# Attention head outputs taken through DRAM to feature rows, softmax sums inverted once per eight heads, in an attention and mixture-of-experts kernel

## The reference, cut to what matters

```python
x = x + attention(layernorm(x))          # x is 2 x 2048 x 256 fp32
x = x + experts(layernorm(x))

def attention(x):                        # 16 heads of 16 features
    Q, K, V = (x @ W.T + b for W, b in (q, k, v))      # split into heads
    A = softmax(Q @ K.T / 4)             # 2048 x 2048 for each of 32 (sequence, head) pairs
    L = local_diffusion_kernel(2048, 0.4)              # a band: |i - j| <= 3, rows sum to 1
    out = (0.6 * A + 0.4 * L) @ V        # heads side by side again: 2048 x 256 a sequence
    return out @ Wo.T + bo

def experts(x):                          # router: 256 -> 512 -> 4, gelu, softmax, the best 2 of 4
    for e in range(4):                   # each token is weighed by its gate of expert e, 0 if not chosen
        out += gate[e] * (gelu(x @ We1[e] + be1[e]) @ We2[e] + be2[e])     # 256 -> 1024 -> 256
```

## Time and profile before

| | |
|---|---|
| median of 3 runs | 1970.37 us (1968.87 to 1970.62) |
| the profiled execution's own time | 1970.84 us |
| its span | 1969.0 us, mean granted TensorE clock 0.996 |
| busy | TensorE 98%, VectorE 83%, ScalarE 68%, GpSimd 18% |

### The profile page before, as it was taken

One profiled execution on the slowest core, in us unless ns is written; L12 is line 12 of the kernel. 1 busy time (PEld: TensorE's weight loads), 2 busy tenths in 40 slices (PEclk: granted clock), 3 DMA queues, 4 the chain that ended last, 5 costly groups with the idle time before them and its releaser, 6 DMA issues. The chain is left out here.

```text
span 1969.0 us, 47293 instructions
## 1 busy us (share of the span) xinstructions
PE 1934.3 (98%) x16220; PEld 1025.6 (52%) x16220; DVE 1642.2 (83%) x2235; ACT 1338.4 (68%) x2374; POOL 346.1 (18%) x379
## 2 busy tenths in 40 slices
PE   7999999999999999999999999999999899999997
PEld 3543333333333333333333333333587799999997
DVE  6799999999999999999999999996156765555554
ACT  3348888888888888888888888888545422223332
POOL 1362010000000010001000000001025622322233
PEclk9999999999999999999999999999999999999999
DMA  8954345434553455435543455342024787888884
GB/s 260 253 121 93 76 97 102 102 75 87 102 112 75 78 102 111 85 75 97 103 101 75 88 101 112 75 78 72 28 71 149 270 253 231 255 250 299 261 273 116
DMA packets 117242, 264.07 MB, mean 134 GB/s; under 512 B 20001, under 2 KB 68257, under 8 KB 110497
## 3 DMA queue, kind: packets, MB, share of 16 engines
q1 hardware_dynamic: 104016, 245.29, 49.4%
q0 software_dynamic: 13152, 17.83, 4.7%
HBM read 206.95 MB, written 73.94 MB: 143 GB/s over the span
## 5 line engine op out<-in xcount | busy, mean ns | idle before, releaser
L618 DVE TENSOR_REDUCE part_max<-psum 128x1 f32<-128x1024 f32 x1024 | 1214.9, 1214 | 13.8 <-PE psum L725 3.2
L686 ACT ACTIVATE probs<-psum 128x512 f32<-128x512 f32 x2048 | 1110.3, 595 | 166.5 <-PE psum L740 108.7
L740 PE MATMUL psum<-score_q,score_k 50*128 50x512 f32 x2048 | 756.9, 448 | 0.1
L725 PE MATMUL psum<-max_k,max_q 48*128 48x512 f32 x2048 | 731.4, 449 | 1.4 <-DVE part_max L618 1.4
L750 PE MATMUL psum<-probs,v_ones 128*32 128x256 f32 x8192 | 654.2, 391 | 0.5 <-ACT probs L686 0.5
L740 PEld LDWEIGHTS psum<-score_q,score_k 50*128 50x128 f32 x2048 | 309.0, 184 | 426.3 <-ACT probs L686 398.1
L750 PEld LDWEIGHTS psum<-probs,v_ones 128*32 128x32 f32 x8192 | 161.2, 108 | 369.9 <-issue 204.4
L725 PEld LDWEIGHTS psum<-max_k,max_q 48*128 48x128 f32 x2048 | 291.2, 185 | 15.8 <-issue 7.0
L1137 ACT ACTIVATE x_sb<-psum,x_sb 128x512 f32<-128x512 f32 (+1 forms) x160 | 101.5, 635 | 254.2 <-PE psum L1517 252.0
L1536 PE MATMUL psum<-w,h_hi 128*128 128x256 f32 x1120 | 202.7, 279 | 0.0
L1536 PEld LDWEIGHTS psum<-w,h_hi 128*128 128x128 f32 x1120 | 179.2, 189 | 10.8 <-issue 0.4
(11 more groups left out here) (177 smaller groups left out, 1301.6 us busy)
## 6 DMA issues: line engine op xcount, KB each, us to landing
w<-w_split SPq DMA_DIRECT2D x40, 2048.0 KB, 8.6
max_q<-qk_pieces SPq DMA_DIRECT2D x192, 128.0 KB, 7.1
score_k<-qk_pieces SPq DMA_DIRECT2D x192, 128.0 KB, 4.6
xs<-in_pads SPq DMA_DIRECT2D x33, 528.0 KB, 7.9
qk_pieces<-pieces SPq DMA_DIRECT2D x32, 512.0 KB, 5.0
w_split<-w_pair SPq DMA_DIRECT2D x32, 512.0 KB, 8.4
max_k<-qk_pieces SPq DMA_DIRECT2D x192, 64.0 KB, 7.8
score_q<-qk_pieces SPq DMA_DIRECT2D x192, 64.0 KB, 2.2
```

What stands on the lines that cost most here:

```text
L618: nc.vector.tensor_reduce(part_max[:, t, p:p + 1], ps_m[p].rearrange("q b f -> q (b f)"), axis=AXIS.X, op=ALU.max).then_inc(m_read, 1)
L686: nc.scalar.activation(probs[kb % 2][:, chunk * BLOCK:(chunk + 1) * BLOCK], score_bank(u, kb, c), ACT.Exp, scale=float(HD) ** -0.5).then_i ...
L725: last = nc.tensor.matmul(ps_m[p][:, h, :], max_q[u][rows, t * P:(t + 1) * P], max_k[u][rows, p * BLOCK:(p + 1) * BLOCK], start=True, stop ...
L740: nc.tensor.matmul(score_bank(u, kb, c), score_k[u][rows, kb * P:(kb + 1) * P], score_q[u][rows, part * BLOCK:(part + 1) * BLOCK], start=T ...
```

## The change

The output bank of a head is no longer transposed. VectorE copies it to `heads_sb` (128 x 512). SyncE stores that to DRAM (`o_raw`) and loads it back with two DMAs: the 16 rows of outputs to 16 partitions of `o_sb`, whose rows are now features (128 partitions, for eight heads, x 2048 queries), and the 16 rows of sums to the same partitions of `sums`. When eight heads are in, VectorE inverts `sums` in place and GpSimd multiplies `o_sb` by it. The factor 0.6 moves into the ones, which become 1/0.6. Three of the four inversions are in heads 9, 17 and 25, in four pieces of 512 columns after tiles 2, 4, 6 and 8. The fourth is in the routing, one piece of 2048 columns. The four matmuls with `jump` for each bank give way to one bf16 matmul of zeros, 32 rows x 512 columns, that opens the bank. VectorE adds the heads to the mixed bank while it takes it out (`add_heads`), where ScalarE copied before. The shift's transposes go in two pieces, after tiles 11 and 12. The queries of Q are no longer permuted, and are stored in runs of 512 elements. The loops over heads of SyncE and VectorE are unrolled.

```diff
-SHIFT_AT = 12
+SHIFT_AT = 11
+GROUP = HEADS // KD
+    INVERT_AT = (2, 4, 6, 8)
...
+def store_out(sp, dram, keep, n):
+    sp.wait_ge(keep["o_copied"], n + 2)
+    sp.dma_start(dram["o_raw"][n], keep["heads_sb"]).then_inc(keep["o_stored"], 16)
+
+def load_out(sp, dram, keep, n):
+    rows = slice((n % GROUP) * HD, (n % GROUP + 1) * HD)
+    sp.wait_ge(keep["o_stored"], 16 * (n + 2))
+    held = n // GROUP
+    if n % GROUP == 0 and held > 0:
+        sp.wait_ge(keep["o_normal"], held)
+    raw = dram["o_raw"][n].rearrange("(j e) q -> e j q", j=BPS)
+    for dst, src in ((keep["o"][rows, n // GROUP, :], raw[0:HD]), (keep["sums"][rows, :], raw[HD:2 * HD])):
+        sp.dma_start(dst.rearrange("p (j q) -> p j q", j=BPS), src).then_inc(keep["o_in"], 16)
+
+def invert_sums(nc, dve, keep, g, piece, pieces):
+    dve.wait_ge(keep["o_in"], 16 * 2 * GROUP * (g + 1))
+    part = keep["sums"][:, piece * SEQ // pieces:(piece + 1) * SEQ // pieces]
+    done = nc.vector.reciprocal(part, part)
...
+def normalise_out(nc, pool, keep, g):
+    pool.wait_ge(keep["o_inverted"], g + 1)
+    heads = keep["o"][:, g, :]
+    nc.gpsimd.tensor_tensor(heads, heads, keep["sums"], ALU.mult).then_inc(keep["o_normal"], 1)
...
-    for t in range(BT):
-        nc.tensor.matmul(out[:, t * P:(t + 1) * P], o[:, kt + t, :], keep["jump"][:], start=t == 0, stop=False)
+    nc.tensor.matmul(out, zeros[:, 0:P], zeros[:, P:P + BLOCK], start=True, stop=False)
...
-                            if qk == 0:
-                                rows = rows.rearrange("p (b j r) -> p j b r", b=BT, j=BPS)
...
# attend, SyncE
-        twice(sp, pairs, body)
+        for n in range(NHEADS):
...
+            if n > 0:
+                store_out(sp, dram, keep, n - 1)
+                load_out(sp, dram, keep, n - 1)
+            if n + 1 < NHEADS:
+                sp.wait_ge(shift_turned, n + 2)
+                load_shift(1 - u)
...
# attend, GpSimd
             split_chunk(n)
-            normalise(n)
             if n + 1 < NHEADS:
                 split_shift(n + 1)
+            if n > GROUP and n % GROUP == 1:
+                normalise_out(nc, pool, keep, n // GROUP - 1)
...
# attend, VectorE
-            nc.vector.transpose(heads_tok[:].rearrange("p t e -> p (t e)"), out_bank(u)).then_inc(heads_turned, 1)
+            nc.vector.tensor_copy(heads_sb, out_bank(u)).then_inc(o_copied, 1)
...
+                if n > GROUP and n % GROUP == 1 and kb in INVERT_AT:
+                    invert_sums(nc, dve, keep, n // GROUP - 1, INVERT_AT.index(kb), len(INVERT_AT))
...
+                    if kb == SHIFT_AT:
...
+                        turn_shift(n + 1, (0, 1))
+                    if kb == SHIFT_AT + 1:
+                        turn_shift(n + 1, (2, 3))
...
# route_and_experts, SyncE: ahead of the constants
+        store_out(sp, dram, keep, NHEADS - 1)
+        load_out(sp, dram, keep, NHEADS - 1)
...
# route_and_experts, GpSimd
+            if i == 1:
+                normalise_out(nc, pool, keep, NHEADS // GROUP - 1)
...
# route_and_experts, VectorE
+        def add_heads(i):
+            b, at = i // BPS, (i % BPS) * BLOCK
+            dve.wait_ge(o_normal, KD * (b + 1))
+            if i > 0:
+                dve.wait_ge(o_ready, i)
+            for m in range(KD):
+                dve.wait_ge(a_ready[m], i + 1)
+                nc.vector.tensor_tensor(attnT[:, m, :], ps_a[m], o_sb[:, KD * b + m, at:at + BLOCK], ALU.add
+                                        ).then_inc(a_copied[m], 1)
...
+        add_heads(0)
         normalise(0)
+        add_heads(1)
...
                 normalise(i + 1)
+                if i + 2 < BLOCKS:
+                    add_heads(i + 2)
+                if i == 0:
+                    invert_sums(nc, dve, keep, NHEADS // GROUP - 1, 0, 1)
```

More of the change, by code:

```diff
@@ L628, in split_shift, with turn_shift, copy_out @@
             dve.wait_ge(shift_step, m + 1)
-        def turn_shift(m):
-            dve.wait_ge(shift_ready, m + 1)
+        def turn_shift(m, quads):
             rows = shift[:].rearrange("p h c t -> p (h c t)").bitcast(F32)
-            for q in range(0, P, QUAD):
-                last = nc.vector.transpose(shift_row[:, q:q + QUAD], rows[q:q + QUAD, :])
-            last.then_inc(shift_turned, 1)
-        def turn_heads(n, u):
-            dve.wait_ge(pv_done, ST * (n + 1) + PV_OPEN)
-            dve.wait_ge(tok_used, n + 1)
-            nc.vector.transpose(heads_tok[:].rearrange("p t e -> p (t e)"), out_bank(u)).then_inc(heads_turned, 1)
-        def invert(n):
-            dve.wait_ge(heads_turned, n + 1)
-            nc.vector.reciprocal(inv_sum[:], heads_tok[:, :, HD]).then_inc(inv_ready, 1)
+            for q in quads:
+                turned = nc.vector.transpose(shift_row[:, q * QUAD:(q + 1) * QUAD], rows[q * QUAD:(q + 1) * QUAD, :])
+            if q == P // QUAD - 1:
+                turned.then_inc(shift_turned, 1)
+        def copy_out(n, u):
+            dve.wait_ge(o_stored, 16 * (n + 1))
+            dve.wait_ge(pv_done, ST * (n + 1) + PV_OPEN)
+            nc.vector.tensor_copy(heads_sb, out_bank(u)).then_inc(o_copied, 1)
         for t in range(ST):
-            maxima(t, t)
+            for p in range(2):
+                maxima(t, t, p)
         split_shift(0)
@@ L1084, in _ @@
     def _(act):
-        def copy_heads(i):
-            for m in range(KD):
-                act.wait_ge(a_ready[m], i + 1)
-                if m == 0 and i > 0:
-                    act.wait_ge(o_ready, i)
-                nc.scalar.activation(attnT[:, m, :], ps_a[m], ACT.Copy).then_inc(a_copied[m], 1)
         def copy_hi(i):
@@ L1098, in exponentials @@
             nc.scalar.activation(prob[:], below_top[:], ACT.Exp).then_inc(exp_ready, 1)
-        for i in range(3):
-            copy_heads(i)
-            if i == 1:
-                copy_hi(0)
+        copy_hi(0)
         def split_x(i):
@@ L1609, in program @@
                 keep["v"] = head_sb("v_sb", [P, BATCH, ST + 2, HEADS, HD])[:]
[L1610 to L1611 removed]
+                keep["o"] = head_sb("o_sb", [P, BATCH * KD, SEQ])[:]
+                keep["sums"] = head_sb("sums", [P, SEQ])[:]
+                keep["heads_sb"] = head_sb("heads_sb", [P, BLOCK])[:]
+                for n in ("o_copied", "o_stored", "o_in", "o_inverted", "o_normal"):
+                    keep[n] = sem(n)
                 for n, toks in (("max_q0", SEQ), ("max_k0", SPLIT)):
```

159 lines of the change are left out of this document (69 added, 90 removed).

## The result

The changed kernel takes 2045.07 us, median of 4 runs (2041.68 to 2052.29), against 1969.78 us of the kernel before on the same chip: a ratio of 1.0387, 95% interval [1.0358, 1.0416]. That is 75 us more where 38 were forecast, above the end of the range (2028).

A forecast was written before the change was run, and what follows sets the result against it. TensorE was taken to set the pace in attention, VectorE close behind. Sum: 1970.84 + 35 (wide inversions) - 4 (other heads) + 1 (DMA) + 6.6 + 0.4 - 7 + 5.9 (routing) = 2008.7, given as 2008 us; range 1998 to 2028.

The forecast's parts named there:

- How late VectorE may be: Attention: 0.55 us of VectorE lateness is free; beyond that each microsecond costs TensorE one, which it can't win back.
- three later pieces of 2.95 us each: Heads 9, 17, 25: pieces after the first, 3.35 us each less 0.4 won back; all four cost 11.65 us a head.
- The reciprocals: VectorE inversions: fixed 153 ns plus 6.25 ns an element, so 3.35 us for 512 and 12.95 for 2048.
- The flat: Rival, 10%: reciprocal time flat in width, 0.68 us for 512 elements; sum 1970 us, the case that isn't slower.
- dearer element: Rival, 15%: slope steeper than 6.25 ns an element; at 8.3 ns a piece takes 4.4 us, total 2025 us.
- the second rival: The dearer element, 15%: 8.3 ns an element, a third above the line, total 2025 us.
- The other heads: Attention's other 28 heads: split shift and copy replacing the transpose save 0.13 us a head, -4 us, between 0 and -6.
- The late shift: SyncE and DMA: shift's load 0.3 us late, +1 us in all; rival, 13%: 2 us in each of three heads, 2013.
- The start of the routing: First projection, behind add_heads(0), a store, two loads and five constants, starts 6.6 us later.
- The mixes: Routing: dropping the matmuls with jump shortens a block by 1.4 us; five blocks, -7 us.
- The inversion in the routing: The 2048-column inversion on VectorE between add_heads(2) and xT_lo(1) delays projection(3): +5.9 us.
- 6.6 + 0.4 - 7 + 5.9: Routing terms: its start, add_heads(1) after the normalised rows in block 1, the mixes, the 2048-column inversion.

The follow-up runs named there:

- after: The changed kernel itself, with four pieces of 512 columns in heads 9, 17 and 25: 2045.07 us, ratio 1.0387 to the kernel before.
- one piece: Changed kernel with only the first 512-column piece whole in heads 9, 17 and 25, the other nine inverting one column: 2005.52 us, ratio 1.0223.
- products: experiment 1 plus three 1024-column VectorE products after tile 2 of heads 9, 17, 25, and four 512-wide reciprocals in head 31: 2025.36 us, measured once.
- experiment 4: Changed kernel with one piece of 128, 256 and 384 columns in heads 9, 17 and 25, the other pieces inverting one column: 1987.15 us, measured once.
- experiment 1: Changed kernel with each of the twelve attention pieces inverting one column only, waits and signals kept, the routing's inversion kept: 1980.3 us, ratio 1.0067.
- 6: experiment 1 with VectorE's wait for the constants moved behind add_heads(0): 1972.84 us, ratio 1.0026.
- experiment 11: experiment 9 with GpSimd's product in the routing waiting until VectorE has made block 2's normalised rows: 1964.84 us, ratio 0.9975; experiment 9 beside it 1965.7 us.
- 7: Experiment 6 with the routing's inversion also cut to one column, so no wide inversion is left: 1967.69 us, ratio 0.9996.
- experiment 9: Experiment 8 with its new tile in bytes given up by the zeros' tile, so later tiles keep their addresses: 1965.22 us, ratio 0.9982; again 1965.7, 0.9987.
- 10: experiment 9 with add_heads(1) moved between the row statistics and the wait for rstd: 1966.21 us, ratio 0.9979.
- 8: Changed kernel, full computation, inverting one row of sums a head as 128 x 16, spread through DRAM; add_heads(0) before the constants' wait: 1972.33 us, ratio 1.0021.

## Why the prediction was wrong, point by point

**The step that failed** stands under "How late VectorE may be": "Beyond that each microsecond of VectorE is one of TensorE". It takes TensorE's pace as fixed. In each of heads 9, 17 and 25 the first wait put the clock from 1.0 to 0.5, and the forecast has no term for that and no rival. The size can be worked out from rows. At the low level a half takes 2.16 us and at the full one 1.24, so a microsecond there loses 1 - 1.24/2.16 = 0.43 us. With the first gap's own 2.9:

| head | low stretch, us | 2.9 + 0.43 x stretch | measured over 39.9 |
|---|---|---|---|
| after, 9 | 47.8 | 23.5 | 23.7 |
| after, 17 | 58.0 | 27.8 | 27.6 (1.3 of it in head 18) |
| after, 25 | 41.0 | 20.5 | 20.9 |
| one piece, 9 | 17.1 | 10.3 | 10.7 |
| one piece, 17 | 3.4 | 4.4 | 4.6 |
| one piece, 25 | 6.8 | 5.8 | 6.4 |
| products, 9 | 30.7 | 16.1 | 16.0 |
| products, 17 | 44.4 | 22.0 | 21.9 |
| products, 25 | 6.8 | 5.8 | 6.7 |

(The products' first gap is 4.30 to 4.42 us, so 3.1 to 3.2 lost; its rows would be 0.2 to 0.3 higher.) Two terms give the three heads of the changed kernel: 8.7 us of first waits and 63.1 of clock, 71.8 of the 72.2 in the profiled execution. That is the slowest run of its kernel, 7 us above the median, so the medians' 65 fit it. The forecast's three later pieces of 2.95 us each hardly appear: at the low clock VectorE has 2.16 us for a reduction of 1.2 and makes them up, and the gap around each is 2.55 us, 0.39 over the others.

**The reciprocals: right.** The price was right to 0.01 us for 512 and 2048 elements. The flat and the dearer element are refuted. The third above the line that the second rival takes, 8.3 ns, and with it the range's end at 2028, was an estimate that no run shows: from 128 to 384 elements (experiment 4) and from 512 to 2048 the runs showed 6.25 ns each.

**The other heads: right.** They are 0.12 and 0.16 us shorter in turn, 0.14 a head for 0.13 forecast, so some -4 us.

**The late shift: right in kind.** Where VectorE is on time (experiment 1) it loses 0.47 to 0.79 us a head, 1.9 us in all for +1 in the sum, far from the 6 of the rival. In the changed kernel itself no such gap stands out: the value groups at that place are as far apart as their neighbours in head 17 (2.16 us) and in head 25 (1.24).

**The start of the routing: the wait right, its consequence not.** +6.4 us for +6.6 up to the first projection. The lower clock behind it (5.42 for 3.69 us) comes on top. By experiments 1 and 6 moving the wait gains 7.5 us for both together, and the next wait for the constants cuts that gain.

**The mixes: too hopeful.** A block of TensorE alone, from projection to projection, takes 15.61 us, and 16.57 before: 0.96 us saved for 1.4. The zero matmuls start the band 0.31 us later, not 0.24. And only three blocks, from projection 3 to 6, are TensorE's alone: -2.9 us for -7.

**The inversion in the routing: right**, 5.1 us for 5.9. The product behind it holds VectorE up for 4.2 us, of which the forecast had nothing. What of that is on the path was not isolated: without the inversion the stretch around the product takes 17.79 us where the next blocks take 15.61, which would be up to 2.2, and experiment 11, which only moves the hold, got 0.85 back.

**The total by medians**: 65 for the pieces, 7.5 for the start, 5.1 for the routing's inversion, and -2.1 for the rest, which is 1967.69 against 1969.78 from runs of two batches and zero by the ratio. That makes 75, and must, as each is the difference of two neighbours in one chain of runs; it doesn't prove the parts. By stage, in the two profiled executions, attention ends 67.6 us later (32 forecast), and from there to the experts it takes 165.6 us instead of 151.5: +14.1, for the forecast's 6.6 + 0.4 - 7 + 5.9 = +5.9. These 14.1 are 6.4 up to the first projection, 3.4 in the next two steps, 7.4 from projection 2 to 3, -2.9 in the three blocks and next to nothing behind them. Six kernels here with this routing code, the changed one among them, take 164.0 to 167.6 us from the last value matmul to the experts, one execution each, so a microsecond or two there tells nothing.

**What stays open** is how long the clock stays low. After the same kind of wait it was 3 to 17 us (one piece), 7 to 44 (products), 41 to 58 (four pieces). Later waits aren't needed for a long stretch, as the products show, and with four pieces all three were long. Nor does a wait always lower it. Ahead of the first projection TensorE waits 1.83 or 1.84 us in seven of these executions alike, and the projection takes 3.69 us in experiments 7, 9 (twice) and 10 but 5.3 to 5.4, at the lower clock, in 6, 8 and 11. Here experiment 9 again, then 11:

```profile
1404.82 3.69 PE L1493 MATMUL psum<-w_o,attnT 128*128 128x256 f32 x16 [1.84 <-DVE attnT L1328]
```

```profile
1404.77 5.38 PE L1494 MATMUL psum<-w_o,attnT 128*128 128x256 f32 x16 [1.84 <-DVE attnT L1329]
```

No run here separates the causes.

## What to carry to other kernels

Where TensorE was full, a wait of it could have two prices in these runs: its length, and the lower clock behind it (0.50 instead of 1.00), which cost up to some 8 times as much (58.0 us x 0.43 against 2.9 to 3.3). Before a burst of another engine's work is put where TensorE can't wait it out, cut it to below what is free there (0.55 us here), or shrink the work itself: the sums needed 16 elements a partition a head and not sixteen copies, and that, with the constants' wait moved, turned +75 us into a kernel 0.1 to 0.2% faster than the one before (experiment 9, intervals [0.9973, 0.9991] and [0.9978, 0.9996]), about the edge of what can be measured. When a profile shows an engine full, read the granted clock of that stretch before taking its pace as given.

## What the runs showed of the hardware that was not expected

- TensorE's clock stayed at the lower level for up to 58.0 us of unbroken work (47.00 busy of 47.00 us at 0.50), and for as little as 3.4 us after the same wait. A lone wait of 2.0 us left it at 1.00, one of 2.9 us didn't; behind several gaps of 1.2 to 1.4 us, one a tile, it was the lower level too. Behind one and the same wait of 1.84 us at the start of the routing it was the lower level in three executions of seven, so the length of a wait alone doesn't decide it.
- A product on GpSimd held up some of VectorE's instructions in SBUF. Beside one of 4.6 us, four TENSOR_SCALAR took 5.66 us instead of 1.38, and a TENSOR_TENSOR of 16 elements with both operands in SBUF took 3.60 instead of 0.2, while an addition with one operand in PSUM (0.64 us), reductions from PSUM (1.2 us) and 32 x 32 transposes in SBUF (0.2 us) were not slowed. What sets the held ones apart, no run here shows.
- RECIPROCAL went by one line from 4 to 2048 elements: 178, 253, 952, 1752, 2552, 3344 and 12945 ns for 4, 16, 128, 256, 384, 512 and 2048.
- A tile of 128 bytes a partition ahead of the experts' went with experts 1.3% slower (406.2 against 401.0 us) with the same instructions and clock, and with the tile elsewhere this was gone in all four executions (experiments 9 to 11).
